# Expert attention: the ScalarE order of "scale the first half of the mixed weights" and "copy the turned input", and where a register is loaded

## The reference, cut to what matters

```python
pooled = hidden_states.mean(axis=1)
logits = relu(pooled @ Wg1 + bg1) @ Wg2 + bg2
vals, idx = top_k(logits, 2)                 # two of four experts for each of the 16 sequences
weights = zeros_like(logits).at[..., idx].set(softmax(vals))
def moe_proj(W, b):                          # the mixed weights of one sequence
    Wc = einsum('be,ecd->bcd', weights, W); bc = weights @ b
    return einsum('btc,bcd->btd', hidden_states, Wc) + bc[:, None, :]
q, k, v = moe_proj(Wq, bq), moe_proj(Wk, bk), moe_proj(Wv, bv)
out = softmax(q k^T / sqrt(16)) v            # 16 heads of 16
return out @ Wo + bo
```

## Time and profile before

| | |
|---|---|
| median of 3 runs | 1201.21 us (1201.0 to 1203.19) |
| the profiled execution, its own time | 1201.55 us |
| its span in the profile | 1199.7 us |
| TensorE matmul busy | 1012.6 us, 84% |
| VectorE busy | 902.4 us, 75% |
| ScalarE busy | 751.6 us, 63% |
| GpSimd busy | 246.2 us, 21% |
| granted TensorE clock, mean | 0.934 of full speed |

### The profile page before, as it was taken

How to read it: one execution, slowest core, us unless ns; L and a number is a source line. 1 busy time by engine, 2 the same in 40 slices (tenths; PEclk the granted TensorE clock), 3 DMA queues, 4 the chain that set the end, 5 groups by cost and what they waited for, 6 DMA issues and landing times. The chain is left out here.

```text
span 1199.7 us, 28144 instructions
## 1 busy us (share of the span) xinstructions
PE 1012.6 (84%) x9206; PEld 822.5 (69%) x9206; DVE 902.4 (75%) x2564; ACT 751.6 (63%) x2800; POOL 246.2 (21%) x467
## 2 busy tenths in 40 slices
PE   3999967578999976667999978999998996798885
PEld 3788854256777753445777758999997984676663
DVE  4888868786888868995777765566656886888884
ACT  2878887577778868885767754112112542788884
POOL 2323210002222212333222310000001122333331
PEclk8999988758999997887999998999998996899998
DMA  7330000000000000004222000000000000000002
GB/s 242 110 126 17 14 1 1 1 9 15 14 13 13 10 2 1 0 0 106 72 83 71 13 2 1 1 0 0 0 1 19 28 28 0 2 2 0 0 1 71
DMA packets 44428, 32.67 MB, mean 27 GB/s; under 512 B 16184, under 2 KB 43456, under 8 KB 44352
## 3 DMA queue, kind: packets, MB, share of 16 engines
q1 hardware_dynamic: 44352, 31.72, 8.8%
HBM read 23.32 MB, written 2.10 MB: 21 GB/s over the span
## 5 line engine op out<-in xcount | busy, mean ns | idle before, releaser
L807 ACT ACTIVATE L1a_pr<-L1a_scores,L1a_nm 128x128 f32<-128x128 f32 x256 | 93.1, 417 | 13.6 <-DVE L1a_nm L885 13.6
L807 ACT ACTIVATE L2a_pr<-L2a_scores,L2a_nm 128x128 f32<-128x128 f32 x256 | 90.9, 392 | 5.8 <-DVE L2a_nm L885 5.8
L807 ACT ACTIVATE L3f_pr<-L3f_scores,L3f_nm 128x128 f32<-128x128 f32 x256 | 90.4, 401 | 3.2 <-DVE L3f_nm L885 3.2
L807 ACT ACTIVATE L0a_pr<-L0a_scores,L0a_nm 128x128 f32<-128x128 f32 x256 | 90.8, 393 | 1.9 <-DVE L0a_nm L885 1.9
L807 ACT ACTIVATION_READ_ACCUMULATOR L1a_pr<-L1a_scores,L1a_nm 128x1 f32 x256 | 65.5, 256 | 0.0
L807 ACT ACTIVATION_READ_ACCUMULATOR L3f_pr<-L3f_scores,L3f_nm 128x1 f32 x256 | 61.7, 241 | 0.0
L885 DVE TENSOR_REDUCE L2a_nm<-L2a_scores 128x4 f32<-128x512 f32 x64 | 42.2, 683 | 25.3 <-PE L2a_scores L654 25.3
L1826 PE MATMUL L2f_inner<-L2f_taT,L2f_loraBT 128*128 128x128 f32 x512 | 59.7, 275 | 0.9 <-DVE L2f_hs L1978 0.9
L1815 PEld LDWEIGHTS L2f_inner<-L2f_xTb,L2f_wiT 128*128 128x128 f32 x512 | 58.3, 192 | 1.5 <-ACT L2f_loraBT L1782 1.2
L1815 PE MATMUL L2f_inner<-L2f_xTb,L2f_wiT 128*128 128x128 f32 x512 | 58.6, 275 | 0.9 <-ACT L2f_loraBT L1782 0.9
L807 ACT ACTIVATION_READ_ACCUMULATOR L0a_pr<-L0a_scores,L0a_nm 128x1 f32 x256 | 59.3, 232 | 0.0
(11 more groups left out here) (603 smaller groups left out, 3066.4 us busy)
## 6 DMA issues: line engine op xcount, KB each, us to landing
setup_ctx_nat<-in_ctx SPq DMA_DIRECT2D x4, 512.0 KB, 5.5
x_all<-in_x SPq DMA_DIRECT2D x1, 2048.0 KB, 12.4
L0a_ctxT<-ctxT_all SPq DMA_DIRECT2D x16, 128.0 KB, 2.0
L_ffn_w_w<-in_L_ffn_w SPq DMA_DIRECT2D x2, 1024.0 KB, 7.1
L1a_ctxT<-ctxT_all SPq DMA_DIRECT2D x16, 128.0 KB, 2.0
L2a_ctxT<-ctxT_all SPq DMA_DIRECT2D x16, 128.0 KB, 2.0
L3a_mem<-in_ctx SPq DMA_DIRECT2D x16, 128.0 KB, 2.0
out<-x_all SPq DMA_DIRECT2D x1, 2048.0 KB, 7.5
```

What stands on the lines that cost most here:

```text
L807: ex = act.activation(pr[q.s][:, j, h, :], S[j][:, h * P:h * P + P], ACT.Exp, bias=nm[q.s][:, j, h:h + 1], scale=-1.0, accum_out=ls[q.s][: ...
```

## The change

In ScalarE's step, `share(new, 0)` stands in front of `copy_x(new)` and no longer behind it. Inside `share`, the wait for `s_v` stands behind the register load and no longer in front of it. Nothing else is changed; the same instructions are issued.

```diff
                 def share(q, n):
-                    if n == 0 and q.earlier(2):
-                        act.wait_ge(s_v[q.earlier(2).s], q.earlier(2).v)
-                    mixing.share(act, q, n)
+                    before = q.earlier(2)
+                    mixing.share(act, q, n, (s_v[before.s], before.v) if n == 0 and before else None)
...
                     mine(prev, 2)
-                    piece(new, copy_x)
                     if mixed_here(new):
                         share(new, 0)
+                    piece(new, copy_x)
                     piece(cur, exp, 0)
...
-    def share(self, act, q, n):
+    def share(self, act, q, n, added=None):
         g, lot = self.g, self.lots[n]
         first = act.value_load(g.chosen[0:1, q.b, 0:1], min_val=0, max_val=3)
+        if added:
+            act.wait_ge(*added)
         act.activation(self.mix[q.s][:, lot], g.experts[:, first, lot], ACT.Copy, scale=g.gates[:, q.b, 0, :]
                        ).then_inc(self.s_share[n][q.s], 1)
```

## The result

The changed kernel has a median of 1200.92 us over 20 runs (1198.05 to 1204.98), the kernel before 1203.15 us over 20 runs on the same chip. The ratio is 0.998, with a 95% interval of 0.9971 to 0.999: 2.4 us faster, between 1.2 and 3.5 (the two medians differ by 2.2). The interval excludes that nothing changed, though the gain is only about the 0.2% that was called measurable. The profiled execution's span is 1196.9 us, against 1199.7.

The account below looks back on a forecast made before the run. ScalarE's order was taken as the bound. Regular steps -2.33, first steps +0.48, +0.2 and +0.8 sum to -0.85 us, from a median of 1201.21 to 1200.4 us; range 1197.9 to 1203.3 us.

Parts of the forecast that it names:

- The ring: Regular step's new cycle, add_v's end, share, copy_x, project_k, add_k, next add_v's end: 10.11 us against the old step's 10.30.
- V to share: From the end of add_v (V) to the share's start on ScalarE, register arithmetic included: 0.16 us.
- add_k to V: VectorE's run from add_k through the normalisation to the end of the next add_v (V), without a wait: 7.28 us.
- Step 13: The last step, ending with the v projection instead of the normalisation: about 9.75 us.
- The first steps: Steps -1 to 2 of L3f, expected to lose time: 0.48, 0, 0.2 and 0.8 us.
- step -1: copy_x follows the share, so project_k of sequence 0 and the first projections come later: +0.48 us.
- step 0: Share done early while ScalarE is idle; the TensorE/VectorE chain of the late gates decides: 0 us.
- step 1: project_k and add_k 0.8 us late, most taken up by VectorE's idle before the gate logits: +0.2 us.
- step 2: project_k later after a longer TensorE wait, possibly running into the lower clock: +0.8 us, between +0.4 and +1.4.
- (a): Rival: the wait costs no register work, add_v's end to share 0.04 us; 2.2 us faster, 1199.0 us; chance 0.12.
- (b): Rival: add_k does not bind and all VectorE's idle time goes; 8.8 us faster, 1192.4 us; chance 0.10.
- (c): Rival: the register load does not run ahead of s_v, share starting later; 6.2 us slower, 1207.4 us; chance 0.10.

Follow-up runs that it names:

- e1: Changed kernel with the wait for s_v put ahead of the register load again: 1207.24 us, ratio 1.0041 to the kernel before.
- e3: Changed kernel with the old order (copy_x, then share) kept in steps -1 to 2: 1199.21 us, ratio 0.9975 to the kernel before.
- e7: Kernel before, copy_x still ahead of share, with only the wait for s_v moved behind the register load: 1202.01 us, ratio 0.9998.
- e2: Register load put ahead of copy_x, copy_x still ahead of the share (load, copy_x, wait, share): 1195.74 us, ratio 0.9947 to the kernel before.
- e4: Changed kernel with the turned input in another bank, so project_k no longer waits for copy_x: 1191.85 us, ratio 0.9914 to the kernel before.
- e6: e2 with the turned input in the other bank as in e4: 1195.45 us, ratio 0.9941 to the kernel before.
- e8: e4 with the wait for s_v ahead of the register load again: 1194.34 us, ratio 0.9928 to the kernel before.

## Why the prediction was right, and where it was off

The forecast was 0.85 us faster, inside a range that held the result. The measured gain, 2.4 us, is almost three times that, and its interval (1.2 to 3.5) leaves 0.85 out. That the time forecast, 1200.4 us, lies so near the 1200.92 measured is luck: I started from a median of 1201.21 over 3 runs, and the kernel before had 1203.15 over 20. A gain of more than 2.4 us had 0.17 of my chances, and of my own 0.68 only 0.03. The mechanism was right and the size too small. By my own terms:

- **The ring.** Right, with each member where I put it, and add_k's wait 0.49 where I said about 0.5; the wait for the scores is 0.16 where I said about 0.3. V to share was 0.15 (I took 0.16), share 1.06 (1.06), copy_x to project_k 0.40 (0.42), project_k to add_k 1.20 (1.19), add_k to V 7.17 (7.28): 9.98 instead of 10.11.
- **The mis-sized term** is add_k to V. I had taken the duration of the normalisation, 0.40, as the time until add_v can start. Without a wait add_v starts 0.31 after it, as the two rows at 1105.76 and 1106.07 show. That is 0.09 of the 0.13, in each of the ten steps with a normalisation. I had used start to start for ScalarE and not here.
- **Step 13** took 9.52, not 9.75. Its ring has no normalisation, and I had let the v projection decide; in the trace add_v doesn't wait there (the row at 1165.50). Another 0.23.
- **Steps 3 to 13** thus gain 3.86 instead of 2.33 us.
- **The first steps** cost 1.50 us, forecast 1.48. The end of add_v is late by 0.47 after step -1 (forecast 0.48), 0.67 after step 0 (0.48), 0.60 after step 1 (0.68) and 1.50 after step 2 (1.48). Step 0's extra 0.2 is in the clock: its scores took 1.44 instead of 1.24 us, at a granted clock of 0.77 instead of 0.90 (e1, with the same order, lost 0.1 there). Step 1 gave 0.07 back instead of costing 0.2. Step 2 cost 0.90 (0.8), with the slower project_k between my two bounds. e3 shows that these costs belong to the order. That the sum came out at 1.50 for 1.48 is partly luck: three steps were off by 0.1 to 0.3 us, and not all the same way.
- **Sum.** -3.86 + 1.50 = -2.36 us, against a measured 2.4 by the ratio. The span fell by 2.8, of which 0.44 is the earlier start of the stage, before anything that was changed.

The rivals. (a), no register work behind the wait, is out: 0.15 us and a row of arithmetic at 1096.5. The load itself began at 1094.9, when the copy of probabilities ahead of it had been released (the turning that it waits for, at 1094.11, lasted 0.60) and not yet started (1094.97). In e7 it stood behind the waiting copy with no wait of its own, and in e2 putting it ahead of that copy took it off the ring. So the rule of the Trainium skill (Advanced Engine Details and Errata, Sequencer Loop), that the sequencer reads on past a waiting instruction, does not hold for a register load behind a waiting copy here. The gain of (a), 2.2 us, lies closer to the measured one than my own, but for another reason: its ring of 9.99 is right in length and wrong in the 0.04 us from V to share. (b), a free add_k, fell with the wait there; e4 shows what it would be, with the bank as the price. (c), a load that doesn't run ahead, is what e1 builds: 10.62 against my 10.75 for it, and slower than before as said, by 4.9 us where I had 6.2.

## What to carry to other kernels

When an instruction is moved in front of another on the same engine, look for who waits for the one that is now second, and close the ring through it: the old ring tells only the upper end of the gain. Look also for the instruction whose wait holds a register load. Ahead of the wrong wait the load gained nothing (e7); ahead of the right one it was worth 0.53 us a step in the old order (e2) and 0.64 in the new (e1 against the changed kernel). For an in-order engine that runs without a wait, sum start to start and not durations.

## What the runs showed of the hardware that I had not expected

The same work, before the stage and in its first steps, took times that differ between these profiles by more than the change is worth. The first turn_x of L3f lies between 1006.93 and 1012.25 us in these ten profiles, though nothing in front of it was changed. And step 0 of L3f, between the ends of add_v, took 11.74 us in e4 and 14.87 in e6, with nearly the same program there; e8, which differs from e4 only in whether the load stands ahead of the wait, took 14.64. Step 0's q projection in e6, and then in e4:

```profile
1025.03 1.92 PE L614 MATMUL L3f_projected<-L3f_xT,mixing_mix 128*128 128x128 f32 x8
```

```profile
1028.60 1.06 PE L614 MATMUL L3f_projected<-L3f_xT,mixing_mix 128*128 128x128 f32 x8
```

The first ran at the lower clock level (granted clock 0.50) and the second at the higher (1.00), both behind TensorE's wait of 2.7 us for the late gates. What decides it was not tried, and with one profile of each kernel it stays open whether the program or the execution does. Executions of one program do differ: in 23 runs of the kernel before the span lay between 1198.3 and 1204.7 us and the mean granted clock between 0.935 and 0.924, lower in the longer ones. It is why the spans of single profiles (1197.7 for e2, 1192.8 for e6) say less than their periods, and why a change of a microsecond or two has to be counted from a fixed instruction inside its stage.
